# Alternating the value and key works of a batch, and loading keys later, in a one-core cross-attention kernel

## The chip, the cores and the metric

The kernel runs on one core of a Trainium2 chip. The metric is the device time of one execution in microseconds (us), as the median of several runs. All stretches and instants below are counted from the start of the span of one profiled execution.

## The reference

Sixteen batches; in each, 100 queries attend to 1444 keys with 16 heads of 8 elements. Queries, keys and values are projected from the inputs with bias and ReLU; keys whose input row sums to zero and queries whose row sums to zero are masked. Cut to what matters:

```python
Q = relu(queries @ Wq + bq); K = relu(keys @ Wk + bk); V = relu(values @ Wv + bv)
scores = einsum('hbqd,hbkd->hbqk', Qh, Kh) / sqrt(dh)      # 16 heads, dh = 8
scores = where(key_mask == 0, -2**32 + 1, scores)
attn = softmax(scores) * q_mask
out = einsum('hbqk,hbkd->hbqd', attn, Vh) + queries        # x: 16 x 100 x 128, context: 16 x 1444 x 128
```

## The kernel before

The order of every engine is written out by hand; semaphores tie the engines together. The names used below:

- **Units and cycles.** A batch has 24 units (12 key tiles of 121 keys, two halves of the heads). Three units make a cycle, so a batch has 8 cycles, numbered 0 to 7. In a cycle TensorE issues the scores of three units ahead (`next_scores`, L670), then the products of three units of exponentials with the values (`value_products`, L694), then one side work. ScalarE does nothing in the loop but the exponentials, one ACTIVATE of 121x800 for each unit (L568). The scores have three PSUM slots, so the scores of unit u wait for the exponential of unit u - 3 (`probs_ready`).
- **Side works.** While batch b is attended, the values of batch b + 1 and the keys of batch b + 2 are projected: four value works V0 to V3 (L614, three key tiles each) and four key works K0 to K3 (L605, 361 columns each). All of them go through one PSUM bank, `work_ps`. A side work therefore waits in `work` until VectorE has read the one before it (`work_free`), and VectorE waits for each (`work_filled`). `SIDE_WORK` gives their order: before, V0 V1 V2 V3 K0 K1 K2 K3, one behind each cycle.
- **VectorE.** It reads each value work (L939, L941), masks it into `values` (three instructions of L951); reads each key work with a running maximum into `k_raw` (L898); and after K3 splits the keys of batch b + 2 into `k_high` and `k_cent` (L917), whose difference `k_low` (L922) it makes in two halves in the next batch. Between these it has per batch: `finish_outputs` (L991 to L1003: normalise the outputs of batch b - 1 and add the residual), `spread_queries` (four instructions of L970 that make `query_bd` of batch b + 1), `finish_keep` (L960, L963), and `turn_outputs` (L979: transpose the accumulated outputs of batch b out of PSUM), which waits for the last product of the batch. The first products of the next batch wait for that transpose (`o_copied`).
- **SyncE** issues the DMAs in one order for each batch: four stores of the outputs of b - 1 (L382, wait for `out_ready`), the load of the keys of batch b + 3 (L358), four loads of the residual (L375), and the replication of `k_high` and `k_low` of batch b + 2 into `k_parts` (L362).
- **Batches.** Batch 0 has an order of its own (`FIRST_SIDE`). Batches 1 and 2 and from 13 on are written out, and batches 3 to 12 run in loops of two batches. Batch 14 has only the four value works (`keys=False`), and batch 15 has no side work. Behind its last value work batch 14 has on VectorE `bound_scores` and `sum_heads` (L927, L931, L1147), and then `turn_outputs(14)`.

Of the kernel before, what the change touches and what calls it, by code (L numbers as in the profile page):

```python
# [17 lines left out]
SLOTS = 4  # L18
# [15 lines left out]
def attention(  # L34
# [34 lines left out]
    VGROUPS = KT // VGROUP  # L69
    KCHUNKS = SKP // BANK  # L70
    KPARTS = 4
    KCOLS = SK // KPARTS
    assert KPARTS * KCOLS == SK and KCHUNKS <= KPARTS
    QB = 4
# [7 lines left out]
    assert SPANS * SPAN == SQ and SPAN <= 32 and HALVES * PAIR * SPANS * 32 == BANK and VCOLS == 32  # L82
    CYCLE = LEAD
    CYCLES = UNITS // CYCLE

# [12 lines left out]
    with ctx:  # L100
# [3 lines left out]
        def sem(name):  # L104
            return ctx.enter_context(nc.semaphore(name))
# [126 lines left out]
        late_replicated = sem("late_replicated")  # L232
# [4 lines left out]
        work_filled = sem("work_filled")  # L237
# [56 lines left out]
        def works_before(b):  # L294

            if isinstance(b, int) and b == 0:
                return 0
            skipped = KPARTS if isinstance(b, int) and b == B - 1 else 0
            return FIRST_WORKS + WORKS * (b - 1) - skipped
# [56 lines left out]
        def _(sp):  # L356
# [76 lines left out]
            def batch(b, parity, load=True, spread=True, late=lambda: None):  # L433

                store(b - 1, 1 - parity)
                if load:
                    sp.wait_ge(work_filled, works_before(b) + VGROUPS)
                    load_keys(b + 3, 1 - parity)
                sp.wait_ge(out_stored, 16 * HALF_PAIRS * b)
                load_residual(b + 1, 1 - parity)  # L440
                late()
                if spread:

                    sp.wait_ge(scores_ready, UNITS * (b + 1))
                    spread_keys(b + 2, parity)
# [150 lines left out]
        def _(pe):  # L596
# [106 lines left out]
            NEXT, AFTER = 1, 2  # L703
            KEYS = tuple((c, AFTER) for c in range(KPARTS))
            VALUES = tuple((KPARTS + g, NEXT) for g in range(VGROUPS))
            SIDE_WORK = VALUES + KEYS
            FIRST_TURNS = ((), (2, 3), (4, 5), (6, 7), (8, 9), (10, 11), (12, 13), (14,))
            assert CYCLES == len(SIDE_WORK) == len(FIRST_TURNS)

# [14 lines left out]
            def first_batch():  # L724

                for cycle in range(CYCLES):
                    units = range(cycle * CYCLE, (cycle + 1) * CYCLE)
# [15 lines left out]
            def batch(b, parity, last=False, keys=True):  # L743
# [7 lines left out]

                for cycle in range(CYCLES):
                    units = range(cycle * CYCLE, (cycle + 1) * CYCLE)
                    for u in units:
                        next_scores(u + LEAD)
                    for u in units:
                        value_products(b, parity, u)
                    k, ahead = SIDE_WORK[cycle]
                    if not last and (keys or ahead == NEXT):
# [120 lines left out]
        def _(dve):  # L880
            v = nc.vector

            def read_keys(b, c, index, before=True):

                step = KCOLS if before else BANK
                at, to = c * step, min((c + 1) * step, SK)
                filled, free, bank = (work_filled, work_free, work_ps) if before else \
                    (first_projected, first_evacuated, psum[:, K_BANKS[c], :])
                if c == 0 and before and isinstance(b, int) and b == 1:

                    dve.wait_ge(first_k_high, FIRST_PIECES)
                    dve.wait_ge(first_k_cent, FIRST_PIECES)
                elif c == 2 and isinstance(b, int) and b == 1 or c == 0 and before:

                    dve.wait_ge(k_high_ready, b)
                    dve.wait_ge(k_cent_ready, b)
                dve.wait_ge(filled, index + 1)
                v.tensor_scalar(k_raw[:, at:to], bank[:, 0:to - at], bk_sb[:], None,  # L898
                                ALU.add, ALU.max, accum_out=k_chunk_max[:, c:c + 1]).then_inc(free, 1)
# [55 lines left out]
            def finish_values(b, parity, g, index):  # L955
                read_values(b, g, index)
                mask_values(b, parity, g, index)

            def finish_keep(b, parity):
                v.tensor_copy(values[0:KTILE, parity, :, :, PAIR * DH],  # L960
                              keep[0:KTILE].unsqueeze(2).to_broadcast([KTILE, KT, PAIRS])).then_inc(v_ready, 1)
                at = slice(b, b + 1) if isinstance(b, int) else bass.ds(b, 1)
                v.tensor_reduce(kept_keys[0:KTILE, at], keep[0:KTILE], AX.X, ALU.add).then_inc(kept_counted, 1)  # L963

            def spread_queries(b, parity):

                src = query_rep[:, :, b * SQ:(b + 1) * SQ] if isinstance(b, int) else \
                    query_rep[:, :, bass.ds(b * SQ, SQ)]
                for t in range(QUADS):
                    ins = v.tensor_tensor(  # L970
                        query_bd[:, parity, t, :].rearrange("p (h q) -> p h q", h=TILE_HEADS),
                        src[:, t].bitcast(F32).unsqueeze(1).to_broadcast([P, TILE_HEADS, SQ]),
                        blockmask[:].unsqueeze(2).to_broadcast([P, TILE_HEADS, SQ]), ALU.mult)
                ins.then_inc(qbd_ready, 1)

            def turn_outputs(b):

                dve.wait_ge(pv_done, UNITS * (b + 1))
                v.transpose(turned.rearrange("p h j g w -> p (h j g w)"), o_ps).then_inc(o_copied, 1)  # L979
# [47 lines left out]
            def split_keys(b, used):  # L1027

                max_keys(b, used)
                dve.wait_ge(k_replicated, 16 * SLOTS * b)  # L1030
                center_keys(k_high, b, k_high_ready)
                center_keys(k_cent, b, k_cent_ready)
# [44 lines left out]
            def batch(b, parity, last=False, keys=True, late=lambda: None):  # L1077
                used = works_before(b)
                if last:
                    finish_outputs(b - 1, 1 - parity)  # L1080
                    return
                for g in range(VGROUPS):
                    finish_values(b + 1, 1 - parity, g, used + g)
                    if g < 2:
                        finish_keys(b + 1, g)
                    elif g == 2:
                        finish_outputs(b - 1, 1 - parity)
                if not isinstance(b, int) or b + 1 >= QB:
                    dve.wait_ge(late_replicated, 16 * SLOTS)
                spread_queries(b + 1, 1 - parity)  # L1090
                finish_keep(b + 1, 1 - parity)
                used = used + VGROUPS
                if keys:
                    for c in range(KPARTS):
                        if c == KPARTS - 1:
                            turn_outputs(b)
                        read_keys(b + 2, c, used + c)
                        if c == 1:
                            late()
                    split_keys(b + 2, used + KPARTS)  # L1100
                else:
                    bound_scores()
                    sum_heads()
                    turn_outputs(b)
# [211 lines left out]
```

## Time and profile before

| | us |
|---|---|
| median of three runs | 355.8 |
| lowest, highest | 355.67, 355.85 |
| the profiled execution | 355.79 |
| its span | 354.1 |

The profiled execution was at full TensorE clock throughout (mean granted share 0.996), and its own time is the median to 0.01 us; 1.7 us of it lie outside the span. The profile gives the busy time of each engine: PE is TensorE's matmuls, PEld its weight loads, DVE is VectorE, ACT is ScalarE, SPq is the queue of SyncE. A row of the timeline merges neighbouring instructions of one kind. It gives the start, the duration, the engine, the line, what is written from what, and the number of instructions; in brackets stands the idle time before it and what ended it.

### The profile page before, as it was taken

The page shows a single profiled execution, that of the slowest core. Times are in us where ns is not written, and L with a number is a line of the kernel's source. Part 1 is how long each engine was busy: PE and PEld are TensorE (multiplying, and loading weights), DVE is VectorE, ACT ScalarE, POOL GpSimd, SP SyncE. Part 2 cuts the span into 40 slices and gives each one's busy share as a digit, 9 for nine tenths or more (in the row PEclk, how much of TensorE's full clock was granted, in tenths as well). Part 3 has the DMA queues.
Part 4 walks back from the last instruction along what each step waited for, and adds up shares of the span by engine and source line. Part 5 has one row for each costly group of instructions (what it writes and reads, how often), then busy time and mean ns, then how long its engine had stood idle before and what let it go on. Part 6 is the DMA issues. An engine that isn't in the chain of part 4 may idle for free.

```text
span 354.1 us, 16749 instructions
## 1 busy us (share of the span) xinstructions
PE 345.4 (98%) x6698; PEld 235.4 (66%) x6698; DVE 236.4 (67%) x777; ACT 299.4 (85%) x395; POOL 4.4 (1%) x28
## 2 busy tenths in 40 slices
PE   7999999999999999999999999999999999999994
PEld 4665676776757677675767767576676767667662
DVE  4789487775848577484867848486784848679321
ACT  1587789888898988889898898989889898989993
POOL 4000000000000000000000000000000000000000
PEclk9999999999999999999999999999999999999998
DMA  7578657777954746384464738447473754537100
GB/s 253 199 256 294 208 189 240 262 228 203 318 136 179 217 149 224 91 292 135 175 201 159 234 91 290 138 169 211 151 239 91 281 149 169 179 109 240 11 10 8
DMA packets 41667, 65.29 MB, mean 184 GB/s; under 512 B 28197, under 2 KB 30758, under 8 KB 41638
## 3 DMA queue, kind: packets, MB, share of 16 engines
q1 hardware_dynamic: 40420, 64.09, 56.2%
q10 hardware_dynamic: 1218, 0.79, 0.8%
q8 instruction: 21, 0.34, 0.4%
q14 instruction: 8, 0.07, 0.1%
HBM read 13.67 MB, written 0.82 MB: 41 GB/s over the span
## 4 chain that ended last, share of the span: by engine, by line
PE 94%; DVE 2%; DMA 2%; issue 1%; ACTq 1%; ACT 0%
PE psum L694 40%; PE psum L670 29%; PE psum L614 12%; PE psum L605 11%; DMA query_rep<-in_xT 2%; PE psum L785 1%; DVE values L951 1%; ACT probs L568 0%; DVE k_low L922 0%; DVE v_biased L941 0%; ACTq L514 0%; ACTq L516 0%; ACTq L518 0%; PE psum L793 0%; DVE flat_mask L1109 0%
## 5 line engine op out<-in xcount | busy, mean ns | idle before, releaser
L568 ACT ACTIVATE probs<-psum 121x800 f32<-121x800 f32 x384 | 293.3, 840 | 37.5 <-PE psum L670 37.5
L694 PE MATMUL psum<-probs,values 121*17 121x200 f32 x3072 | 154.8, 334 | 0.0
L670 PEld LDWEIGHTS psum<-query_bd,k_parts 64*121 64x121 f32 x1536 | 91.7, 181 | 50.8 <-ACT probs L568 35.0
L670 PE MATMUL psum<-query_bd,k_parts 64*121 64x200 f32 x1536 | 115.5, 281 | 0.3 <-ACT probs L568 0.2
L694 PEld LDWEIGHTS psum<-probs,values 121*17 121x17 f32 x3072 | 78.0, 97 | 41.3 <-issue 1.7
L898 DVE TENSOR_SCALAR_CACHE_REDUCE k_raw<-psum,bk_sb 128x361 f32<-128x361 f32 (+2 forms) x63 | 37.3, 593 | 53.9 <-PE psum L605 53.8
L614 PE MATMUL psum<-wv_sb,keyT 128*32 128x129 f32 (+1 forms) x1536 | 53.8, 273 | 0.1
L605 PE MATMUL psum<-keyT,wk_mixed 128*32 128x361 f32 (+2 forms) x504 | 51.3, 481 | 1.2 <-DVE flat_mask L1109 0.6
L614 PEld LDWEIGHTS psum<-wv_sb,keyT 128*32 128x32 f32 (+1 forms) x1536 | 43.7, 108 | 6.4 <-DVE v_biased L941 0.5
L951 DVE TENSOR_SCALAR values<-v_biased,keep 121x128 f32<-121x128 f32 x192 | 43.3, 283 | 6.1
L941 DVE TENSOR_TENSOR v_biased<-psum,bv_sb 121x384 f32<-121x384 f32 x64 | 35.0, 548 | 0.0
L922 DVE TENSOR_TENSOR k_low<-k_cent,k_high 128x722 fp32r<-128x722 f32 (+3 forms) x33 | 29.2, 884 | 0.3
L979 DVE STREAM_TRANSPOSE turned_sb<-psum 128x512 f32<-128x512 f32 x15 | 10.8, 717 | 22.4 <-PE psum L694 22.4
L605 PEld LDWEIGHTS psum<-keyT,wk_mixed 128*32 128x32 f32 x504 | 15.9, 112 | 9.5 <-issue 3.6
L970 DVE TENSOR_TENSOR query_bd<-query_rep,blockmask 128x200 fp32r<-128x200 f32 x60 | 17.9, 362 | 0.0
L917 DVE TENSOR_SCALAR k_high<-k_raw,k_max 128x1444 fp32r<-128x1444 f32 (+3 forms) x18 | 16.0, 889 | 1.7 <-DVE k_max L911 0.2
L917 DVE TENSOR_SCALAR k_cent<-k_raw,k_max 128x1444 f32<-128x1444 f32 (+3 forms) x18 | 15.9, 884 | 0.0
L939 DVE TENSOR_SCALAR keep<-psum 121x3 f32<-121x3 f32 x64 | 10.1, 158 | 7.0 <-PE psum L614 7.0
L526 ACT ACTIVATE queryT<-psum,bq_sb 128x400 f32<-128x400 f32 x3 | 1.8, 603 | 6.3 <-PE psum L785 6.3
L1010 DVE STREAM_TRANSPOSE turned_sb<-psum 128x256 f32<-128x256 f32 x2 | 0.9, 449 | 8.2 <-PE psum L694 8.2
L983 DVE TENSOR_TENSOR o_norm<-turned_sb,inv_den 128x64 f32<-128x64 f32 x32 | 5.9, 222 | 0.6
L898 DVE DVE_READ_ACCUMULATOR k_raw<-psum,bk_sb 128x1 f32 x63 | 5.3, 84 | 0.0
(77 smaller groups left out, 64.0 us busy)
## 6 DMA issues: line engine op xcount, KB each, us to landing
k_parts<-k_high SPq DMA_DIRECT2D x30, 722.0 KB, 4.8
k_parts<-k_low SPq DMA_DIRECT2D x30, 722.0 KB, 5.4
keyT<-in_ctxT SPq DMA_DIRECT2D x15, 722.0 KB, 4.2
query_rep<-late_high SPq DMA_DIRECT2D x2, 600.0 KB, 3.8
query_rep<-late_low SPq DMA_DIRECT2D x2, 600.0 KB, 4.2
residual<-in_x SPq DMA_DIRECT2D x64, 12.5 KB
out<-residual SPq DMA_DIRECT2D x60, 12.5 KB
k_parts<-k_high SPq DMA_DIRECT2D x2, 359.0 KB, 3.4
```

The source lines that it names most:

```text
L568: nc.scalar.activation(probs[0:KTILE, u % PROB_SLOTS], scores_ps[0:KTILE, u % SCORE_SLOTS, :, 0:QCOLS], ACT.Exp, scale=SCALE).then_inc(pro ...
L605: mm = nc.tensor.matmul(bank[m:m + VCOLS, 0:to - at], wk_mixed[:, m:m + VCOLS], keyT[:, parity, at:to], start=True, stop=True)
L614: mm = nc.tensor.matmul(bank[m:end, n * VW:(n + 1) * VW], keyT[:, parity, at + m:at + end], wv_sb[:], start=True, stop=True)
L670: mm = nc.tensor.matmul(scores_ps[0:KTILE, u % SCORE_SLOTS, j, n * TCOLS:(n + 1) * TCOLS], k_parts[rows, parity, t, kt * KTILE:(kt + 1) * ...
L694: mm = nc.tensor.matmul(spans[c * VCOLS:c * VCOLS + VUSED, half, :, :, 0:SPAN], values[0:KTILE, parity, kt, half * HALF_PAIRS + c, 0:VUSED ...
L898: v.tensor_scalar(k_raw[:, at:to], bank[:, 0:to - at], bk_sb[:], None, ALU.add, ALU.max, accum_out=k_chunk_max[:, c:c + 1]).then_inc(free, 1)
L917: v.tensor_scalar(target[:, at], k_raw[:, at], 0.0, of_batch(k_max, b), ALU.max, ALU.subtract).then_inc(done, 1)
L922: v.tensor_tensor(k_low[:, at], k_cent[:, at], k_high[:, at].bitcast(F32), ALU.subtract).then_inc(done, 1)
L941: v.tensor_tensor(v_biased[0:KTILE, g], work[:, :, 0:D], bv_sb[0:KTILE].unsqueeze(1).to_broadcast([KTILE, VGROUP, D]), ALU.add).then_inc(f ...
L951: v.tensor_scalar(values[0:KTILE, parity, kt, :, 0:PAIR * DH], v_biased[0:KTILE, g, n].rearrange("p (a w) -> p a w", w=PAIR * DH), 0.0, ke ...
L970: ins = v.tensor_tensor(query_bd[:, parity, t, :].rearrange("p (h q) -> p h q", h=TILE_HEADS), src[:, t].bitcast(F32).unsqueeze(1).to_broa ...
L979: v.transpose(turned.rearrange("p h j g w -> p (h j g w)"), o_ps).then_inc(o_copied, 1)
```

## The change

Three things move, and nothing is computed otherwise. The side works alternate, V0 K0 V1 K1 V2 K2 V3 K3. VectorE's reads follow that order, and its other steps are placed among them anew. The load of the keys of batch b + 3 waits for the seventh side work of the batch (V3, behind cycle 6) where it waited for the fourth (V3, behind cycle 3).

```diff
-                    sp.wait_ge(work_filled, works_before(b) + VGROUPS)
+                    sp.wait_ge(work_filled, works_before(b) + 2 * VGROUPS - 1)
                     load_keys(b + 3, 1 - parity)
...
-            SIDE_WORK = VALUES + KEYS
+            SIDE_WORK = tuple(work for pair in zip(VALUES, KEYS) for work in pair)
...
                 for g in range(VGROUPS):
-                    finish_values(b + 1, 1 - parity, g, used + g)
+                    finish_values(b + 1, 1 - parity, g, used)
+                    used = used + 1
                     if g < 2:
                         finish_keys(b + 1, g)
                     elif g == 2:
                         finish_outputs(b - 1, 1 - parity)
-                if not isinstance(b, int) or b + 1 >= QB:
-                    dve.wait_ge(late_replicated, 16 * SLOTS)
-                spread_queries(b + 1, 1 - parity)
-                finish_keep(b + 1, 1 - parity)
-                used = used + VGROUPS
+                        if not isinstance(b, int) or b + 1 >= QB:
+                            dve.wait_ge(late_replicated, 16 * SLOTS)
+                        spread_queries(b + 1, 1 - parity)
+                    else:
+                        finish_keep(b + 1, 1 - parity)
+                    if keys:
+                        if g == VGROUPS - 1:
+                            turn_outputs(b)
+                        read_keys(b + 2, g, used)
+                        used = used + 1
+                        if g == 2:
+                            late()
                 if keys:
-                    for c in range(KPARTS):
-                        if c == KPARTS - 1:
-                            turn_outputs(b)
-                        read_keys(b + 2, c, used + c)
-                        if c == 1:
-                            late()
-                    split_keys(b + 2, used + KPARTS)
+                    split_keys(b + 2, used)
                 else:
                     bound_scores()
                     sum_heads()
```

The changed file has one more line, so the lines of the loop are numbered one higher in it. Two places follow, as the program orders them.

VectorE in batch 13, from the read of V2 on. The kernel before has the outputs, V3, the spreading of the queries (L970), `finish_keep` and then the key reads:

```order
L939 TENSOR_SCALAR keep<-psum 121x3
L941 TENSOR_TENSOR v_biased<-psum,bv_sb 121x384
L951 TENSOR_SCALAR values<-v_biased,keep 121x8x16 x3
L991 TENSOR_SCALAR inv_den<-turned_sb 128x16
L993 RECIPROCAL inv_den<-inv_den 128x16
L996 TENSOR_TENSOR inv_den<-inv_den,row_mask 128x16
L983 TENSOR_TENSOR o_norm<-turned_sb,inv_den 128x2x4x8 x2
L1003 TENSOR_TENSOR residual<-residual,o_norm 128x128
L939 TENSOR_SCALAR keep<-psum 121x3
L941 TENSOR_TENSOR v_biased<-psum,bv_sb 121x384
L951 TENSOR_SCALAR values<-v_biased,keep 121x8x16 x3
L970 TENSOR_TENSOR query_bd<-query_rep,blockmask 128x200 x4
```

VectorE at the same place of the changed kernel; L971 spreads the queries, and L899 reads K2:

```order
L940 TENSOR_SCALAR keep<-psum 121x3
L942 TENSOR_TENSOR v_biased<-psum,bv_sb 121x384
L952 TENSOR_SCALAR values<-v_biased,keep 121x8x16 x3
L992 TENSOR_SCALAR inv_den<-turned_sb 128x16
L994 RECIPROCAL inv_den<-inv_den 128x16
L997 TENSOR_TENSOR inv_den<-inv_den,row_mask 128x16
L984 TENSOR_TENSOR o_norm<-turned_sb,inv_den 128x2x4x8 x2
L1004 TENSOR_TENSOR residual<-residual,o_norm 128x128
L971 TENSOR_TENSOR query_bd<-query_rep,blockmask 128x200 x4
L899 TENSOR_SCALAR k_raw,k_chunk_max<-psum,bk_sb 128x361
L940 TENSOR_SCALAR keep<-psum 121x3
```

Between the value works V2 and V3 there is now a key read, and the outputs and the spreading both stand ahead of it.

VectorE in batch 14 of the changed kernel, from the spreading to the transpose of the outputs. In the kernel before the rows from `keep` to the transpose are the same, and only the spreading stands behind the value read in place of ahead of it; but there the value read is of a work behind cycle 3, and here of one behind cycle 6:

```order
L971 TENSOR_TENSOR query_bd<-query_rep,blockmask 128x200 x4
L940 TENSOR_SCALAR keep<-psum 121x3
L942 TENSOR_TENSOR v_biased<-psum,bv_sb 121x384
L952 TENSOR_SCALAR values<-v_biased,keep 121x8x16 x3
L961 COPY values<-keep 121x96
L964 TENSOR_REDUCE kept_keys<-keep 121x1
L928 TENSOR_REDUCE q_max<-queryT 128x16
L932 TENSOR_TENSOR bound_terms<-k_max,q_max 128x16
L1150 TENSOR_REDUCE head_sum<-quad_base 128x16
L980 STREAM_TRANSPOSE turned_sb<-psum 128x512
```

The steps between the last value read and the transpose did not move against each other; their place against TensorE's cycles did.

## Rows read from the trace of the kernel before

**Rows 1.** The page, busy time of each engine, and the chain that ended last.
```profile
PE 345.4 (98%) x6698; PEld 235.4 (66%) x6698; DVE 236.4 (67%) x777; ACT 299.4 (85%) x395; POOL 4.4 (1%) x28
...
PE 94%; DVE 2%; DMA 2%; issue 1%; ACTq 1%; ACT 0%
```
**Rows 2.** Timeline of TensorE in batch 6, from V2 to K1.
```profile
154.51 0.84 PE L614 MATMUL psum<-wv_sb,keyT 128*32 128x129 f32 x24
...
157.13 0.84 PE L614 MATMUL psum<-wv_sb,keyT 128*32 128x129 f32 x24
...
158.71 1.21 PE L694 MATMUL psum<-probs,values 121*17 121x200 f32 x24
...
159.74 0.79 PE L605 MATMUL psum<-keyT,wk_mixed 128*32 128x361 f32 x8
160.46 0.71 PEld L670 LDWEIGHTS psum<-query_bd,k_parts 64*121 64x121 f32 x12 [0.59 <-ACT probs L568]
...
162.30 0.79 PE L605 MATMUL psum<-keyT,wk_mixed 128*32 128x361 f32 x8
```
**Rows 3.** Timeline of ScalarE in the same batch, one cycle.
```profile
160.96 2.30 ACT L568 ACTIVATE probs<-psum 121x800 f32<-121x800 f32 x3 [0.27 <-PE psum L670]
```
**Rows 4.** Timeline of VectorE in the same batch, from V2's read on.
```profile
155.42 0.16 DVE L939 TENSOR_SCALAR keep<-psum 121x3 f32<-121x3 f32 x1 [0.38 <-PE psum L614]
...
158.16 0.16 DVE L939 TENSOR_SCALAR keep<-psum 121x3 f32<-121x3 f32 x1
...
159.49 1.19 DVE L970 TENSOR_TENSOR query_bd<-query_rep,blockmask 128x200 fp32r<-128x200 f32 x4
...
160.59 0.26 DVE L960 COPY values<-keep 121x96 f32<-121x96 f32 x1
...
160.78 0.59 DVE L898 TENSOR_SCALAR_CACHE_REDUCE k_raw<-psum,bk_sb 128x361 f32<-128x361 f32 x1
```
**Rows 5.** Timeline: V3's read in batch 1; V2 and V3's read in batch 5.
```profile
54.55 0.15 DVE L939 TENSOR_SCALAR keep<-psum 121x3 f32<-121x3 f32 x1
...
133.81 0.84 PE L614 MATMUL psum<-wv_sb,keyT 128*32 128x129 f32 x24
...
137.55 0.15 DVE L939 TENSOR_SCALAR keep<-psum 121x3 f32<-121x3 f32 x1
```
**Rows 6.** Timeline of batch 0: the end of a key read, and TensorE's next key work.
```profile
37.93 0.09 DVE L898 DVE_READ_ACCUMULATOR k_raw<-psum,bk_sb 128x1 f32 x1
...
38.07 0.16 PEld L605 LDWEIGHTS psum<-keyT,wk_mixed 128*32 128x32 f32 x8 [0.19 <-DVE k_raw L898]
```
**Rows 7.** SyncE's queue in batch 6; then the landing times of the key loads, 57 to 300 us.
```profile
158.43 3.90 SPq L382 DMA_DIRECT2D out<-residual  x4
...
162.63 0.36 SPq L358 DMA_DIRECT2D keyT<-in_ctxT  x1
...
DMA to landing us min/median/max: 4.0/4.2/5.2
```
**Rows 8.** Timeline of batch 14 from V3 on, and the turn of its outputs.
```profile
322.75 0.84 PE L614 MATMUL psum<-wv_sb,keyT 128*32 128x129 f32 x24
...
323.53 0.88 PE L670 MATMUL psum<-query_bd,k_parts 64*121 64x200 f32 x12
...
324.03 24.32 ACT L568 ACTIVATE probs<-psum 121x800 f32<-121x800 f32 x33 [0.31 <-PE psum L670]
...
326.31 1.81 DVE L927 TENSOR_REDUCE q_max<-queryT 128x16 f32<-128x1600 f32 x1
...
326.77 1.21 PE L694 MATMUL psum<-probs,values 121*17 121x200 f32 x24
327.91 1.12 PE L670 MATMUL psum<-query_bd,k_parts 64*121 64x200 f32 x12
...
328.25 0.28 DVE L1147 TENSOR_REDUCE head_sum<-quad_base 128x16 f32<-128x128 f32 x1
...
332.43 0.72 DVE L979 STREAM_TRANSPOSE turned_sb<-psum 128x512 f32<-128x512 f32 x1 [3.90 <-PE psum L694]
```

More of the change, by code:

```diff
@@ L84, in attention @@
     CYCLES = UNITS // CYCLE
+    assert KPARTS == VGROUPS
     Q_BANKS = (3, 6, 6)
```

## The prediction

> **What bounds the kernel now.** I read the page first, then the timeline of one loop batch engine by engine, then the end of the kernel. On the page [rows 1] TensorE's matmuls fill 98% of the span and make up 94% of the chain that ended last; ScalarE is at 85%, VectorE at 67%. The reader is to see next, in the timeline of batch 6 [rows 2], that TensorE steps without a gap: V2 at 154.51, V3 at 157.13, K0 at 159.74, K1 at 162.30. A cycle that holds a value work lasts 2.61 us, one that holds a key work 2.56 us, so four of each make 20.68; the V2 works of batches 5 and 6 [rows 2, 5] are 20.70 apart. ScalarE [rows 3] works 2.30 us for each cycle and then idles 0.27 until TensorE brings new scores: it is led by TensorE. The 0.59 that the weight loads idle "for probs" [rows 2] is no wait of the engine, since the matmuls of the work before are still running then (159.74 + 0.79 = 160.53, past the 160.46 at which the scores begin). So in batches 1 to 13 each piece that delays TensorE is paid in full, and nothing that VectorE or the DMAs do earlier gains anything. Only from V3 of batch 14 on is it otherwise: ScalarE runs 33 exponentials in 24.32 us without a break [rows 8], 2.21 for each cycle, and leads.
>
> **The order of the works itself** costs nothing in batches 1 to 13: a cycle costs 2.61 or 2.56 by what it holds, and scores and products lie between any two side works before and after. There are still four of each.
>
> **The read of K2** is the first term. All side works share one bank, so V3 can start only when K2 has been read. I count from V2's start on TensorE. V3 is due two cycles later, 2.61 + 2.56 = 5.17. VectorE reads V2, masks it and finishes the outputs; in batch 6 it gets to the next instruction at 158.16 - 154.51 = 3.65 [rows 2, 4]. Now four spreading instructions come next, 1.10 us (159.49 to 160.59) [rows 4], and only then the read of K2, 0.59 (160.78) [rows 4]. TensorE's first weight load comes 0.05 behind the end of such a read (37.93 + 0.09 = 38.02, then 38.07) [rows 6]; with what a weight load usually has as a lead I take 0.07. That is 5.41 against 5.17: TensorE stands still for 0.24. In batch 5 VectorE gets there at 137.55 - 133.81 = 3.74 [rows 5], which gives 0.33, and in the written-out batch 1 at about 3.55 (54.55, with V2 five periods of 20.70 ahead of 154.51) [rows 2, 5], which gives 0.14. Five batches of the loops behave as batch 6, five as batch 5, and 1, 2 and 13 as batch 1: 5 x 0.24 + 5 x 0.33 + 3 x 0.14 = 3.3 us. In the loops the spreading also has register work ahead of each instruction, which so far lay under the masks of V3 and now follows a wait; the trace doesn't show it there. Its bounds are nothing and 0.1 per loop batch, the spread between batches 5 and 6; I take a quarter, 0.2 in all. **Sum: 3.5, bounds 3.3 and 4.3.** Nothing takes the stall back, as ScalarE idles already.
>
> **The other reads** are in time. V1 needs K0 read, V2 needs K1 read: the value read begins 0.91 behind its work (154.51 to 155.42) [rows 2, 4], the masks and half a `k_low` follow while TensorE is at scores and products, the key work is complete only at 2.61 + 0.79 = 3.40, is read by about 4.1 (0.59) [rows 4] and must be read by 5.17. The cover is 1 us. K3, the transpose and the splitting of the keys keep their place at the end of the batch, and so does V0's read behind them. V3's values must be ready for the first products of the next batch; in batch 14 VectorE is past them 2.46 behind V3's start, as counted below, and they are wanted there at 4.02.
>
> **The key load** costs nothing, by a margin that has to be counted. In SyncE's queue it stands behind four stores, which wait for the outputs; these are finished behind V2 before and after. In batch 6 the stores take 158.43 to 162.33 and the load is issued at 162.63 [rows 7], 8.12 behind V2, and not when its own wait is over. The new wait, V3's end, comes at 5.41 + 0.9 = 6.3 and so ends earlier too. The load lands 4.0 to 5.2 after issue, median 4.2 [rows 7]: at 12.3, at worst 13.3. The keys are now wanted by K0 of the next batch, at 5.41 + 2.61 + 2.56 + 2.61 = 13.2. Queued behind the load are the residual's loads and the replication of `k_high`, which so goes out some time after `k_high` is ready, and `k_low`'s goes out one cycle later than before. Both are wanted only by the scores of cycle 7 of the next batch. Price: 0 at the median, bounds 0 and 0.1 per batch.
>
> **Batch 14** is the second term, in two parts. First, its value works now stand behind cycles 0, 2, 4 and 6, with empty cycles between. Before, a value cycle is 2.61 and an empty one 2.21, 4.82 for a pair. After: from the scores at s (323.53) [rows 8] the products of the following empty cycle start at s + 3.24 (326.77), since the third scores wait for a slot that ScalarE frees; then 1.03 of products (158.71 to 159.74) [rows 2] and 0.78 of value work (322.75 to 323.53) [rows 8] until the next scores: 5.05. With three score slots ScalarE cannot be fed ahead for the long cycle. Three pairs x 0.23 = **0.7 us**. Second, the transpose of batch 14's outputs. VectorE reaches `q_max` 3.56 behind V3 (326.31 - 322.75), of which 1.10 is spreading that now lies ahead: 2.46. The bound's steps last until 328.53, 2.22 more; with 0.72 for the transpose (332.43) it is ready at 5.40 and the first products of batch 15 can start at 5.47 behind V3. Without it they would start at 0.78 + 3.24 = 4.02. Before, the transpose had 3.90 us of idle time ahead of it [rows 8]; that cover is gone, as V3 moved from cycle 3 to cycle 6. TensorE stands for 1.45. The scores behind it (1.14 after the start of the products, 326.77 to 327.91) would have been just in time for ScalarE, so nearly all of it comes through: **1.4 us**. Batch 15 has nothing to win it back with.
>
> **Sum:** 3.5 + 0.7 + 1.4 = 5.6 on the profiled 355.79, which is the median: 361.4.
>
> **A rule against the reading.** In the trace, matmuls are at 98% but the weight loads at 66% [rows 1]. The Trainium skill, page "Perfetto Trace Analysis", section "Identifying the Most-Contended Engine", says that matmul busy time is a poor measure of TensorE's headroom and the share of its weight loads a better one. By it a third of TensorE would be spare and would take up a late read. What ScalarE's 0.27 before every group shows [rows 3] speaks against that here.
>
> **Rivals.**
> *The stalls of batches 1 to 13 are taken up.* If TensorE had room in its cycles, K2's late read would vanish in it, and only batch 14 would pay: 355.8 + 2.1 = 357.9. For it speaks the gap between the two shares [rows 1]; against it that equal works follow at equal distances of 2.61 and 2.56, and that in batch 0 a late read of a key work did make the weight loads wait, 0.19 [rows 6]. If the end hides too, it is 355.8.
> *The mixture gains.* Where long and short cycles alternate, the longer sum could set the pair in place of each cycle's own maximum: in batch 14 TensorE has 2.61 + (2.61 - 0.78) = 4.44 for a pair and ScalarE 4.42, against 4.82 now. Over four pairs that is 1.5 us, and with no stall at K2 the time is 354.3. It decides if ScalarE can be fed ahead and if VectorE is through with the spreading 0.24 us earlier than I count. The slot that holds the third scores back speaks against it: products 3.24 behind the scores in an empty cycle [rows 8]. The Trainium skill, page "Perfetto Trace Analysis", section "Optimization Strategy", advises just this, to interleave stretches whose most contended engine differs; in batches 1 to 13 both kinds have the same one.
> *The keys come late.* At the longest landing, 5.2, and with an issue at 8.3, the keys land at 13.5, some 0.4 past what K0 wants with its weight loads ahead; in eleven batches this adds 4.5: 366.
> *The queue of SyncE hides the edit.* The load of keys may start at the same point relative to the stores as before, as I expect; this alone is worth nothing either way.
>
> **How the numbers follow.** Chances: my forecast, with its own range of 360.0 to 363.0, 0.76; stalls taken up, 357.9, 0.08 (a third of it with the end hidden too, 355.8); the mixture gains, 354.3, 0.05; keys late, 366, 0.07; the rest, 0.04, is the first term with a milder end, 359. The range is 357.8 to 363.8; outside are the gain, the hidden end and the late keys, 0.15. About 0.2%, 0.7 us, is what a measurement of this kernel can tell from no change. Faster by more: 0.05; within: 0.03; slower by more: 0.92.
>
> **What would show it.** In the timeline after, V3 should start 5.4 to 5.5 behind V2 in the loops with "<-DVE k_raw" ahead of its weight loads, 0.14 less in the written-out batches; batches should be 20.9 to 21.1 long; K0 should start 2.61 behind V0 without waiting for `keyT`. In batch 14 the value works should be 5.0 apart, and the first products of batch 15 should wait for the transpose. The prediction is wrong if V2 to V3 is 5.17, if TensorE waits for a key load, or if the value works of batch 14 are 4.4 to 4.8 apart.

## The result, and the profile after

The changed kernel takes 363.85 us, the median of four runs between 362.7 and 364.7. The kernel before, run beside it on the same chip, takes 355.74. The ratio is 1.023, with a 95% interval of 1.021 to 1.025. The change costs 8.1 us where 5.6 was forecast, and the time lies just above the range's end of 363.8. The profiled execution took 363.6 with a span of 361.8, against a span of 354.1 before. Medians in this document are of all runs of a kernel; two kernels, K2 first and batch 14 alone, had one slow run each, and without it their medians are 362.11 and 357.53.

The page of the changed kernel, busy time of each engine and the chain that ended last, answers to [rows 1]:

```profile
PE 348.6 (96%) x6698; PEld 234.7 (65%) x6698; DVE 236.9 (65%) x777; ACT 299.4 (83%) x395; POOL 4.4 (1%) x28
...
PE 77%; DVE 12%; issue 5%; ACT 1%; DMA 1%; ACTq 1%; DVEq 1%
```

The busy times of VectorE and ScalarE moved by 0.5 us at most, so the added time is waiting, except 3.2 us more on TensorE's matmuls, a part of which comes back below as a lower clock. VectorE had 2% of the chain before and has 12% now: it is what TensorE waited for in the added time.

The waits of the changed kernel are next, each with its total in us, how often it came and the longest:

```profile
DVE keep L940 <- PE psum L615: 70.6, 43, 2.8
ACT probs L569 <- PE psum L671: 46.1, 117, 2.3
...
PEld psum L615 <- DVE k_raw L899: 6.1, 13, 0.5
...
DVE values L952 <- issue: 2.6, 1, 2.6
...
PEld psum L695 <- DVE values L961: 1.9, 1, 1.9
```

The third row is the late read of K2: thirteen value works, one in each of batches 1 to 13, waited for a key read. The fourth and the fifth are one event each, and no step of the prediction has them.

**The loop.** Timeline of batch 6 in the changed kernel, from V2 to V3, with ScalarE's and SyncE's rows of the same stretch:

```profile
159.97 0.85 PE L615 MATMUL psum<-wv_sb,keyT 128*32 128x129 f32 x24
...
162.59 0.79 PE L606 MATMUL psum<-keyT,wk_mixed 128*32 128x361 f32 x8
...
163.63 1.19 DVE L971 TENSOR_TENSOR query_bd<-query_rep,blockmask 128x200 fp32r<-128x200 f32 x4
163.81 2.30 ACT L569 ACTIVATE probs<-psum 121x800 f32<-121x800 f32 x3 [0.26 <-PE psum L671]
...
164.73 0.59 DVE L899 TENSOR_SCALAR_CACHE_REDUCE k_raw<-psum,bk_sb 128x361 f32<-128x361 f32 x1
...
165.38 0.59 PEld L615 LDWEIGHTS psum<-wv_sb,keyT 128*32 128x32 f32 x24 [0.45 <-DVE k_raw L899]
165.38 0.86 PE L615 MATMUL psum<-wv_sb,keyT 128*32 128x129 f32 x24
...
163.89 3.90 SPq L383 DMA_DIRECT2D out<-residual  x4
168.10 0.36 SPq L359 DMA_DIRECT2D keyT<-in_ctxT  x1
```

V3 starts 165.38 - 159.97 = 5.41 us behind V2, where it was due at 5.17. The bracket on its weight loads names the cause. In batch 5 the distance is 5.50 and in batch 13 it is 5.31. The key load goes out 168.10 - 159.97 = 8.13 behind V2, and no weight load of a key work waited for it. Behind the late V3 ScalarE idles for 0.65 us where it idled for 0.26: the stall is passed on to it. Batches 3 to 12 are 21.05 and 20.95 long in turn, batches 1 and 2 are 20.86.

**Batch 13.** Timeline of the changed kernel around its end, VectorE and TensorE:

```profile
313.17 0.16 DVE L940 TENSOR_SCALAR keep<-psum 121x3 f32<-121x3 f32 x1 [0.99 <-PE psum L615]
...
313.91 0.29 DVE L952 TENSOR_SCALAR values<-v_biased,keep 121x128 f32<-121x128 f32 x1
...
316.79 0.48 DVE L952 TENSOR_SCALAR values<-v_biased,keep 121x128 f32<-121x128 f32 x2 [2.60 <-issue]
317.19 0.25 DVE L961 COPY values<-keep 121x96 f32<-121x96 f32 x1
...
317.38 0.71 DVE L980 STREAM_TRANSPOSE turned_sb<-psum 128x512 f32<-128x512 f32 x1
...
314.87 0.79 PE L606 MATMUL psum<-keyT,wk_mixed 128*32 128x361 f32 x8
315.59 0.88 PE L671 MATMUL psum<-query_bd,k_parts 64*121 64x200 f32 x12
318.19 1.21 PE L695 MATMUL psum<-probs,values 121*17 121x200 f32 x24 [1.72 <-DVE values L961]
319.20 0.86 PE L615 MATMUL psum<-wv_sb,keyT 128*32 128x129 f32 x24
```

Between the first and the second mask of V3's values VectorE does nothing for 2.60 us, and the profile names no releaser ("issue"). All that stands behind the masks is late with them, and so is the transpose of batch 13's outputs. Batch 14's first products wait in the program for both, the finished values and the transpose. The bracket names the copy into the values (L961), but that ended at 317.44; the transpose ended at 318.09, and the products start 0.10 behind it, the distance at which they follow the transpose in batch 15 too. So V0 of batch 14 starts 4.34 behind K3 (314.87 to 319.20) and not 2.56: 1.78 us lost at one place.

**The end.** Timeline of the changed kernel from V3 of batch 14 on:

```profile
334.36 0.84 PE L615 MATMUL psum<-wv_sb,keyT 128*32 128x129 f32 x24
...
336.79 1.81 DVE L928 TENSOR_REDUCE q_max<-queryT 128x16 f32<-128x1600 f32 x1
...
338.92 0.71 DVE L980 STREAM_TRANSPOSE turned_sb<-psum 128x512 f32<-128x512 f32 x1
...
339.73 1.98 PE L695 MATMUL psum<-probs,values 121*17 121x200 f32 x24 [1.28 <-issue]
...
341.64 1.54 PE L671 MATMUL psum<-query_bd,k_parts 64*121 64x200 f32 x12
342.41 1.57 ACT L569 ACTIVATE probs<-psum 121x800 f32<-121x800 f32 x2 [2.29 <-PE psum L671]
```

The first products of batch 15 start 339.73 - 334.36 = 5.37 behind V3 and right behind the transpose. But they then take 1.98 us where 24 such matmuls took 1.21 before [rows 8], and the twelve scores behind them 1.54 for 0.88. Four stretches of 1 us show why; behind the busy shares of the engines stand the granted clock, the DMA share and GB/s:

```profile
339.00:340.00 1.00, 0.27 (x8) 0.26 (x12) 0.93 (x4) 1.00 (x2) 0.00 (x0) 1.00 0.14 13
340.00:341.00 1.00, 1.00 (x20) 0.69 (x15) 0.90 (x5) 0.12 (x1) 0.00 (x0) 0.51 0.19 18
341.00:342.00 1.00, 1.00 (x15) 0.36 (x4) 0.07 (x1) 0.00 (x0) 0.00 (x0) 0.50 0.22 20
342.00:343.00 1.00, 1.00 (x12) 0.93 (x10) 0.00 (x0) 0.59 (x1) 0.00 (x0) 0.50 0.15 14
```

Just behind the 1.28 us of idle time TensorE was granted half its clock, the 1.2 GHz level, for about 3 us.

**The sum of the two traces.** V0 of batch 1 starts 0.91 earlier in the profiled execution after; over the executions profiled here this start lies between 44.85 and 46.10, and in one at 49.03. From there to V0 of batch 13 the changed kernel takes 3.29 more, over batch 13 1.92 more (0.14 for K2 and 1.78 for the gap), and from V0 of batch 14 to the end 3.44 more. -0.91 + 3.29 + 1.92 + 3.44 = 7.7, the difference of the spans.

### The profile page after: what moved, and what is told of

It reads as the page before. It is cut to its first block, busy times and chain, and to the rows that moved or that the text cites. A ratio compares the mean times of both kernels' runs of the same rounds, so it can differ in the third digit from the quotient of the medians.

```text
span 361.8 us, 16749 instructions
## 1 busy us (share of the span) xinstructions
PE 348.6 (96%) x6698; PEld 234.7 (65%) x6698; DVE 236.9 (65%) x777; ACT 299.4 (83%) x395; POOL 4.4 (1%) x28
## 4 chain that ended last, share of the span: by engine, by line
PE 77%; DVE 12%; issue 5%; ACT 1%; DMA 1%; ACTq 1%; DVEq 1%
PE psum L695 32%; PE psum L671 23%; PE psum L615 12%; PE psum L606 9%; DVE values L952 3%; DVE query_bd L971 2%; DVE v_biased L942 2%; ACT probs L569 1%; DVE k_raw L899 1%; DMA query_rep<-in_xT 1%; PE psum L786 1%; DVE o_norm L984 1%; DVE inv_den L994 1%; DVE inv_den L997 1%; DVEq L971 0%
## 5 line engine op out<-in xcount | busy, mean ns | idle before, releaser
L615 PEld LDWEIGHTS psum<-wv_sb,keyT 128*32 128x32 f32 (+1 forms) x1536 | 42.4, 108 | 11.1 <-DVE k_raw L899 6.1
L899 DVE TENSOR_SCALAR_CACHE_REDUCE k_raw<-psum,bk_sb 128x361 f32<-128x361 f32 (+2 forms) x63 | 37.2, 592 | 11.4 <-PE psum L606 11.3
L971 DVE TENSOR_TENSOR query_bd<-query_rep,blockmask 128x200 fp32r<-128x200 f32 x60 | 17.9, 360 | 0.0
L899 DVE DVE_READ_ACCUMULATOR k_raw<-psum,bk_sb 128x1 f32 x63 | 5.2, 83 | 0.0
```

What stands on the lines that cost most here:

```text
L615: mm = nc.tensor.matmul(bank[m:end, n * VW:(n + 1) * VW], keyT[:, parity, at + m:at + end], wv_sb[:], start=True, stop=True)
L971: ins = v.tensor_tensor(query_bd[:, parity, t, :].rearrange("p (h q) -> p h q", h=TILE_HEADS), src[:, t].bitcast(F32).unsqueeze(1).to_broa ...
```

## The experiments

Three terms have to be told apart: K2's late read, the end, and the gap in batch 13. Each expectation stands as it was written before its run. Line numbers of the experiments are up to two higher than before.

**The changed kernel again.** No edit. Is the gap a matter of one execution, or of the program?

> The changed kernel once more. In its profiled execution the loop batches paid what the prediction says (V2 to V3 2.79 and 2.89 us in place of 5.17 - 2.61 = 2.56), but three things were not in the sum: VectorE stood 2.6 us between two mask instructions of V3 in batch 13, TensorE ran at half clock for 3.6 us after its wait for the transpose in batch 15, and batch 1 began 0.9 us earlier. Theory A, the gap belongs to a place in VectorE's code (the 44th record behind the loop's branch, in both kernels) and the clock to the wait: both come again at the same place, and the time is 362.5 to 364.7. Theory B, both are accidents of one execution: they are gone or elsewhere, and the span is about 3 us shorter.

Measured: 363.42, ratio 1.020 (1.013 to 1.027), against 356.04 beside it. The gap stands at the same instruction, 2.48 us long, and K3 to V0 takes 4.21, so it belongs to the program. The low clock doesn't: here the same products follow the same idle time at full speed, as the timeline and the stretch of this execution show.

```profile
340.10 1.21 PE L695 MATMUL psum<-probs,values 121*17 121x200 f32 x24 [1.28 <-issue]
341.24 0.88 PE L671 MATMUL psum<-query_bd,k_parts 64*121 64x200 f32 x12
...
340.00:341.00 1.00, 0.90 (x24) 0.69 (x24) 0.86 (x6) 0.50 (x1) 0.00 (x0) 1.00 0.18 16
```

From V0 of batch 14 to the end it took 2.26 more than before, against 3.44 in the first: the clock was worth 1.2 us there. The eight runs of the changed kernel fall into two groups by their mean granted clock. Three at 0.996 to 0.998 took 362.7 to 363.3, five at 0.992 to 0.994 took 363.6 to 364.7. That the lower clock of the five is this one at the end isn't shown, as only the profiled executions show the place; its size fits.

**K2 read ahead of the spreading.**

```diff
                     elif g == 2:
                         finish_outputs(b - 1, 1 - parity)
+                        if keys:
+                            read_keys(b + 2, g, used)
+                            used = used + 1
                         if not isinstance(b, int) or b + 1 >= QB:
                             dve.wait_ge(late_replicated, 16 * SLOTS)
                         spread_queries(b + 1, 1 - parity)
+                        if keys:
+                            late()
                     else:
                         finish_keep(b + 1, 1 - parity)
-                    if keys:
+                    if keys and g != 2:
                         if g == VGROUPS - 1:
                             turn_outputs(b)
                         read_keys(b + 2, g, used)
                         used = used + 1
-                        if g == 2:
-                            late()
```

> VectorE reads K2 between finish_outputs and spread_queries in place of behind both; all else as in the changed kernel. My theory: K2 is then read at 3.65 + 0.59 = 4.25 to 4.35 behind V2, ahead of the 5.17 at which V3 is due, so V2 to V3 is 5.17 in batches 1 to 13 and the batches are 20.70 long: 3.5 us less than the changed kernel, about 360.3. Rival, TensorE is held by something else in that cycle (the later replication of the keys, the order of the works itself): less than 1 us changes.

Measured: 362.28, ratio 1.014 (1.004 to 1.024). Batches 1 to 12 are 20.70 long, as before the change, and V3 stands 5.17 behind V2: the read was the whole cause of the longer batches. Yet the time fell by only 1.1 to 1.6 us and not by 3.4, and the 360.3 that I expected was missed. The gap is still at that mask, now 2.90 long, so more of it comes through. Timeline of this kernel, and the stretch from 315 to 317 us:

```profile
315.33 2.20 PE L695 MATMUL psum<-probs,values 121*17 121x200 f32 x24 [2.01 <-DVE values L961]
317.28 1.47 PE L615 MATMUL psum<-wv_sb,keyT 128*32 128x129 f32 x24
...
315.00:317.00 2.00, 1.67 (x24) 1.02 (x28) 1.90 (x6) 0.31 (x1) 0.00 (x0) 0.53 0.16 15
```

K3 to V0 is 5.56 here and V0 to V1 5.67, with the clock at half from shortly before the end of a wait of 2.01 us on. In the two traces of the changed kernel that wait was 1.72 and 1.59, and the clock stayed full behind it. Against 4.34 and 5.06 in the changed kernel that takes back 1.8 of the 3.4.

**The transpose ahead of the bound**, in batch 14 alone, where the bound's steps held it up. This is the whole edit.

```diff
                 else:
+                    turn_outputs(b)
                     bound_scores()
                     sum_heads()
-                    turn_outputs(b)
```

> In batch 14 VectorE makes the transpose of the outputs ahead of bound_scores and sum_heads; all else as in the changed kernel. My theory: the first products of batch 15 no longer wait (1.4 us), TensorE doesn't stand still and its granted clock stays at full level, which gives back another 1.2 to 1.4: 2.7 us less than the changed kernel, about 361.1. Rival 1, the clock falls anyway: 1.4 less. Rival 2, ScalarE's queue had hidden the wait: nothing.

Measured: 361.62, ratio 1.016 (1.008 to 1.024), 1.8 to 2.2 below the changed kernel, where I had expected 2.7. Its timeline, with V3 at 334.98:

```profile
337.85 0.72 DVE L980 STREAM_TRANSPOSE turned_sb<-psum 128x512 f32<-128x512 f32 x1 [0.35 <-PE psum L695]
...
339.00 1.21 PE L695 MATMUL psum<-probs,values 121*17 121x200 f32 x24
```

The products follow V3 by 4.02, the time that the prediction gave them without the transpose, with no idle time and at full clock. From V0 of batch 14 to the end the trace is 0.76 above the kernel before: that is the other part of the end, the value works 5.05 apart.

**Batch 14 alone.** The kernel before, with the value works of batch 14 behind cycles 0, 2, 4 and 6 and the spreading ahead of V3's read there.

```diff
-                    k, ahead = SIDE_WORK[cycle]
+                    k, ahead = SIDE_WORK[cycle] if keys else (VALUES[cycle // 2] if cycle % 2 == 0 else KEYS[0])
...
```

> The kernel before, with only batch 14's value works behind cycles 0, 2, 4 and 6 (and the spreading of the queries ahead of V3's read there); keys and loads as before. My theory: value works 5.05 apart costs 0.7, the transpose 1.4, the clock behind it 1.2 to 1.4: 3.4 us more than the kernel before, 359.2. Rival, the tail was dear only for what batch 13 did to it: 0.7 to 2.1 more, 356.5 to 357.9.

Measured: 357.65, ratio 1.005 (1.002 to 1.008), 1.6 us above the kernel before, with the value works 5.04 apart. I had expected 3.4 more, clock included; the median has less than half of that, and it is the rival's range of 0.7 to 2.1 that holds. The profiled execution, 359.28, had the low clock behind the same idle time, and from V0 of batch 14 to the end it took 3.4 more than before. This is the end without anything else.

**The late load alone.** The kernel before, with one line of the change.

```diff
-                    sp.wait_ge(work_filled, works_before(b) + VGROUPS)
+                    sp.wait_ge(work_filled, works_before(b) + 2 * VGROUPS - 1)
```

> The kernel before, with only the load of the keys waiting for the seventh side work of the batch (here K2) in place of the fourth. My theory: the keys are wanted by the first key work of the next batch, behind cycle 4, so nothing waits; batches stay 20.70 long and the time is that of the kernel before, within 0.3 us. Rival: the later load meets the replication of k_high and makes TensorE wait for k_parts: batches longer than 20.75.

Measured: 355.55, ratio 0.9985 (0.996 to 1.001). In its batch 6 the load goes out 11.37 behind V2, 3.2 later than before, and it costs nothing. But in this order K0 stands behind cycle 4 of the next batch, and in the changed order behind cycle 1, so the run doesn't test whether the keys come late there. The changed kernel's own rows do: its load goes out as early as before, and no key work waits.

**Four fills ahead of batch 13.** The rows of batch 13 leave it open what VectorE waited for. One kind of DMA traffic comes at that time, the packets of queue 14, called "instruction". The view of DMA queues has this row for 313 to 319 us after, and the next for 306 to 310 us before; the third is from the timeline of the kernel before in that stretch:

```profile
q14 instruction: 2, 0.02, 1.0%
```

```profile
q14 instruction: 2, 0.02, 1.4%
...
308.79 0.60 DVE L898 TENSOR_SCALAR_CACHE_REDUCE k_raw<-psum,bk_sb 128x361 f32<-128x361 f32 x1 [2.55 <-PE psum L605]
```

So the kernel before has the packets too, just where VectorE waited 2.55 us ahead of K1's read. In batches 1 to 12 that wait is 1.68 to 1.84, as in batch 6:

```profile
163.16 0.59 DVE L898 TENSOR_SCALAR_CACHE_REDUCE k_raw<-psum,bk_sb 128x361 f32<-128x361 f32 x1 [1.78 <-PE psum L605]
```

In both kernels the long pause ends ahead of the 45th record of VectorE in the trace behind the last loop's branch (register and branch instructions counted). And in all nine profiled executions without added instructions, of both kernels and of the experiments, it ends 1.7 to 1.9 us behind the start of the first of these packets. The reading is that the code behind the loop has to be brought in, at a place in the program. Fills move that place:

```diff
+        pad = sb("pad", [P, 4])
...
+                if isinstance(b, int) and b == B - 3:
+                    for n in range(4):
+                        v.memset(pad[:, n:n + 1], 0.0)
                 for g in range(VGROUPS):
                     finish_values(b + 1, 1 - parity, g, used)
```

> The changed kernel with four one-column memsets on VectorE at the start of batch 13. My theory: VectorE's gap belongs to a place in the code, behind the 44th record past the loop's branch, so it moves up by four instructions: from between two masks of V3 to ahead of V3's read. Most of it then lies where VectorE waits for V3 anyway; K3 starts 0.5 to 1.2 late and V0 of batch 14 follows K3 at 2.56 to 2.8 in place of 4.2 to 4.3: 0.6 to 1.2 us less than the changed kernel. Rival, the gap is tied to the step (V3's masks) or to the DMAs at that time: it stays behind V3's first mask, and the time doesn't change.

Measured: 361.33, ratio 1.015 (1.011 to 1.019), faster by 2.1 to 2.5 than the changed kernel although it does more. Timeline of batch 13 in it, then the queue's row for 311 to 315 us:

```profile
313.86 0.16 DVE L941 TENSOR_SCALAR keep<-psum 121x3 f32<-121x3 f32 x1 [0.99 <-PE psum L616]
...
314.59 0.68 DVE L953 TENSOR_SCALAR values<-v_biased,keep 121x128 f32<-121x128 f32 x3
...
315.80 0.72 DVE L981 STREAM_TRANSPOSE turned_sb<-psum 128x512 f32<-128x512 f32 x1 [0.34 <-PE psum L696]
...
315.55 0.79 PE L607 MATMUL psum<-keyT,wk_mixed 128*32 128x361 f32 x8
...
317.08 1.21 PE L696 MATMUL psum<-probs,values 121*17 121x200 f32 x24
318.11 0.84 PE L616 MATMUL psum<-wv_sb,keyT 128*32 128x129 f32 x24
...
q14 instruction: 2, 0.02, 1.6%
```

The three masks are one unbroken row, and K3 to V0 is 2.56. These rows also give the cover of the transpose, the time that it may be late without anybody waiting: it idles for 0.34, ends at 316.52, and the products start at 317.08, of which 0.10 is the usual distance. That is 0.8 us, and 2.60 - 0.8 = 1.8 is what the changed kernel lost. The first of the two packets begins 2.05 ahead of V3's read (311.81); in the changed kernel it begins 1.80 behind it (314.97). My expectation had the gap move to another open place at a cost of 0.5 to 1.2; it was covered wholly. By the 1.7 to 1.9 us above, the pause is over before V3 can be read.

**Two fills.** The same with `range(2)`.

> The changed kernel with two one-column fills on VectorE at the start of batch 13 where the run with four had four. With four, the instruction packet that comes in just behind the gap in the changed kernel landed 3.8 us earlier against the work around it, and the gap was covered by the wait for TensorE. If the gap belongs to a place in VectorE's code, two fills move it by about two instructions: ahead of the biasing or the first mask of the fourth value read of batch 13, behind a keep read or a wait of 0.99 us that covers a part of it at most, so that 0.7 to 1.8 us of it stay: median 362.5 to 363.6, and no third fetch anywhere. If it belongs to a time (a neighbour's traffic, the load of the next batch), the gap stays at the same instruction as without fills, with 2.6 us and the median of 363.4 to 363.9. If any fill takes it away altogether, as four did, the median is 361.3 and how the code lies against the packets matters more than the count.

Measured: 361.41, ratio 1.0145 (1.011 to 1.019). Two act as four: the first packet comes 1.98 ahead of V3's read and nothing is left open. A cause tied to the time or to the key load is hard to hold with that, since nothing but VectorE's code changed. The count of instructions, which I had taken for the measure, falls as well: with half the fills the packets moved as far.

**The mended kernel.** Alternation in batches 1 to 13 with K2 read ahead of the spreading, the late load, batch 14's works behind cycles 0 to 3, and the transpose ahead of the bound.

```diff
-                    k, ahead = SIDE_WORK[cycle]
+                    k, ahead = SIDE_WORK[cycle] if keys else (VALUES + KEYS)[cycle]
...
```

The rest of the edit is that of K2 first and of the transpose first.

> The changed kernel with K2 read ahead of the spreading, the transpose of batch 14 ahead of the bound, and the value works of batch 14 behind cycles 0 to 3 as before; batches 1 to 13 alternate. My theory: batches 1 to 12 are 20.70 long, the end costs what it did in the kernel before, and only VectorE's gap in batch 13 is left, 2.1 us, with 0 to 1 for the clock behind it: 357.9 to 358.9. Rival, some cost belongs to the alternation itself: batches longer than 20.70, or over 359.

Measured: 357.88, ratio 1.006 (1.004 to 1.009). All batches up to 12 are 20.70, the end is as before, and the view of waits has the gap:

```profile
DVE values L952 <- issue: 2.9, 1, 2.9
```

K3 to V0 is 4.60, which is 2.04 lost, and 2.87 less the cover of 0.8 is 2.1. The profiled execution itself began some 3 us late and is no typical one; the median is from ten runs.

**Alternation in the loops only.** Batches 1 to 12 as in the mended kernel, batches 13 and 14 as before the change.

```diff
+                    apart = isinstance(b, int) and b >= B - 3
+                    k, ahead = (VALUES + KEYS)[cycle] if apart else SIDE_WORK[cycle]
...
```

The rest gives VectorE the matching order in each part.

> Batches 1 to 12 alternate with K2 read ahead of the spreading; batches 13 and 14 have the order of the kernel before. My theory: nothing is left to pay, since the batches are 20.70 long and the gap in batch 13 lies ahead of the read of K1 as in the kernel before, where VectorE has 2 us to wait: the time of the kernel before, within 0.5 us. Rival 1, alternation gains on its own: less than 355. Rival 2, it costs on its own: over 356.5.

Measured: 355.43, ratio 0.9993 (0.998 to 1.001). The gap is there, 2.41 us, ahead of K1's read of batch 13 as in the kernel before, and it is covered there.

**The mended kernel with four fills.**

> The mended order (alternation, K2 read ahead of spreading, batch 14 with its value works behind cycles 0 to 3, transpose ahead of the bound) with the four fills at the start of batch 13. Without the fills it was at 357.9, 2.1 to 2.3 us above the kernel before, with a gap of 2.87 us at a mask of batch 13 and the fourth key work to the first value work of batch 14 4.60 apart. If that gap is all that is left between the two kernels: no gap of over 2.2 us in the open in batch 13, its works 2.56 to 2.61 apart throughout, and a median of 355.6 to 356.2, the kernel before within 0.2 per cent. If something else is left: above 356.8. If the gap only moves to another uncovered place: 357 to 358.5.

Measured: 355.83, ratio 0.9995 (0.998 to 1.001). Its page:

```profile
PE 345.3 (97%) x6698; PEld 235.2 (66%) x6698; DVE 236.8 (67%) x781; ACT 299.2 (84%) x395; POOL 4.5 (1%) x28
...
PE 93%; DVE 2%; DMA 2%; issue 1%; ACTq 1%; ACT 0%
```

This is the page of the kernel before, with four instructions more. The fills alone took off 357.88 - 355.83 = 2.05 us. With all three terms gone, the alternating order of batches 1 to 13 and the late load together cost nothing, and they bring nothing.

## Why the prediction was right and wrong

**What bounds the kernel: right.** In batches 1 to 13 each delay of TensorE came through in full: batches longer by 0.25, 0.35 or 0.16 with nothing given back, and ScalarE, idle for 0.26 in batch 6 as before [rows 3], idles for 0.65 behind the stall. The weight loads' share is 65%, so the rule of the Trainium skill, page "Perfetto Trace Analysis", section "Identifying the Most-Contended Engine", would still see a third of TensorE to spare. The measurement decides against reading it that way here, and the rival that the stalls are taken up falls.

**The read of K2: right.** Predicted 5.41, 5.50 and 5.31 behind V2 in batches 6, 5 and 13; measured 5.41, 5.50 and 5.31. The term was 3.5; the traces show 3.29 + 0.14 = 3.4, and the run with K2 read first removes it.

**The load and the other reads: right.** The issue was put 8.12 behind V2 and came 8.13 behind, so the new wait moved nothing, as expected. No key work waited for its keys, and the last run, with the late load in it, is at the time of the kernel before. The rival of late keys falls.

**Alternation itself: right, it costs nothing.** The rival that the mixture gains falls too: with no stall left, batches are 20.70 and not shorter. The advice of the Trainium skill, page "Perfetto Trace Analysis", section "Optimization Strategy", to interleave stretches with different most contended engines has nothing to work on in batches 1 to 13, and in batch 14, where the engines differ, the mixture is 0.76 us slower.

**Batch 14: right in size, and one step is missing.** The value works were put 5.05 apart and are 5.05 apart; the first products of batch 15 were put 5.47 behind V3 and came at 5.37. The two parts were to cost 0.7 and 1.4 and cost 2.1 to 2.3 together in the three traces without the clock's fall; 0.76 is left with the second removed. Missing is what an idle time of 1.28 us can do to TensorE's clock. Six profiled executions have it; in three of them (the changed kernel, K2 first, batch 14 alone) the clock was granted at half behind it, worth 1.2 us, and in three not. The prediction reckoned the stall at the engine's full speed on both sides.

**The step that failed** is the one that I made in a subordinate clause: "K3, the transpose and the splitting of the keys keep their place at the end of the batch, and so does V0's read behind them. V3's values must be ready for the first products of the next batch". In that I gave V3's values a cover of about 1.5 us (4.02 - 2.46) and asked only what VectorE's own instructions take from it. Two things are wrong with it. The transpose keeps its place at the end, but V3's read and masks now stand right ahead of it, and the first products wait for it too; its cover is 0.8 us, not 1.5. And in batch 13 VectorE pauses at those masks for 2.60 us, a term that the sum put at nothing. Before, V3 was read three works earlier, and the pause lay ahead of K1's read, where VectorE waits anyway, at no cost. It now cost 1.78 and 1.65 in the two traces of the changed kernel, and 2.0 to 2.5 in the medians.

With the pause covered the changed kernel takes 361.33 and 361.41, and the forecast was 361.4. That the two agree so closely is in part luck. The medians fell by more than the traces' 1.7, and the clock is the likely rest. The clock's fall is in no term either, and seven of the eight runs with fills had a mean granted clock of 0.997 or more, against two of eight without. The sum of what was measured is 3.4 for K2, 2.1 to 2.3 for the end and 1.65 to 1.78 for the gap, together 7.2 to 7.5. The three runs with the higher clock lie 7.0 to 7.5 above the kernel before, and the clock of the other five makes up the rest of 8.1.

The row that would have warned was in the timeline of the kernel before: in batch 13 K1's read had waited 2.55 where batches 1 to 12 wait 1.7 to 1.8. The prediction took batch 13 for one like batch 1 and counted nothing in it.

**What stays open.** That VectorE waits for its code is argued from the packets, from the fixed place, and from the fills; no row names it as releaser. How the place follows from the program isn't settled, since two fills moved the packets as far as four; no run put fills at another place or on another engine. Nor is it known why the clock fell in some executions and not in others. The length of the idle time alone doesn't tell: in batch 13 it stayed full behind 1.58, 1.59, 1.72 and 1.99 us in four executions, and fell with 2.01 in one.

## What to carry to other kernels

A change of order moves not only work but also cover, that of steps that keep their place too. For each step that gets a nearer deadline, look for the longest pause of its engine in that part of the program, in written-out code behind a loop above all, and not only for the work ahead of it; a pause that costs nothing today is a price for whoever is moved into it. When a sum comes out near the measured time everywhere but at one instruction, a few idle instructions ahead of that place are a cheap test of whether the code's layout is what was measured. And when an instruction waits for two things, look at the ends of both: the bracket names one. Last, an alternation of works on one shared buffer makes each reader's delay hit the very next work, so all that stands ahead of a read has to be counted anew.

## What the runs showed of the hardware

VectorE stood still for 2.4 to 2.9 us in the first written-out batch behind a loop, in each of nine profiled executions ahead of the 45th record behind the branch. The stop ended 1.7 to 1.9 us behind the start of a packet of the queue called "instruction". Where it fell on a wait for TensorE, 1.7 to 1.8 us of it would have been spent anyway. Two or four fills of 0.06 us each at the start of that batch took 2 us off the time. And TensorE's granted clock fell to half at an idle time of 2.01 us, and behind one of 1.28 us in three executions, while it stayed full behind the same 1.28 us in three others and behind 1.58 to 1.99 us in four.
